# Four-layer graph network on one core: the product of negative mean and inverse root moves from VectorE to GpSimd

## The reference

```
h = max(layernorm(x), 0); x = x + L0(h, adj)   # normed = layernorm(h)*g1+be1; 8-head masked softmax(n n^T) n;
                                               # then x' = h + that; y = layernorm(x')*g2+be2; x' + gelu(y W1 + b1) W2 + b2
h = max(layernorm(x), 0); x = x + L1(h, adj)   # graph attention, 4 heads, leaky relu, masked softmax
h = max(layernorm(x), 0); x = x + L2(h, adj)   # the same form with other weights
h = max(layernorm(x), 0); x = x + L3(h, adj)   # q, k, v attention, 4 heads, Wo, relu
```

## Time and profile before

| | |
|---|---|
| time, median of 3 runs | 4204.97 us (4204.6 to 4206.16) |
| the profiled execution: time, span | 4209.86 us, 4208.1 us |
| busy: PE, DVE, ACT, POOL | 3984.2, 3210.8, 2121.9, 408.2 us (95%, 76%, 50%, 10%) |
| TensorE's granted clock over the span | 0.99 |
| one period, 2106.88 to 2233.52 us | 126.64 us, of which PE busy 123.19, DVE 99.68, ACT 66.26, POOL 12.79 |
| groups on GpSimd: `ve`, `rs`, `amx` | 192 x 514 ns, 192 x 1460 ns, 64 x 401 ns |
| VectorE's `nb` | 192 x 143 ns |

### The profile page before, as it was taken

How to read it: one execution, slowest core, us unless ns; L and a number is a source line. 1 busy time by engine, 2 the same in 40 slices (tenths; PEclk the granted TensorE clock), 3 DMA queues, 4 the chain that set the end, 5 groups by cost and what they waited for, 6 DMA issues and landing times.

```text
span 4208.1 us, 78701 instructions
## 1 busy us (share of the span) xinstructions
PE 3984.2 (95%) x32868; PEld 2119.6 (50%) x32868; DVE 3210.8 (76%) x6281; ACT 2121.9 (50%) x3297; POOL 408.2 (10%) x465
## 2 busy tenths in 40 slices
PE   5799999999999999999999999999999999999997
PEld 2455555455555455554555554555554555554553
DVE  5677778877777877777877777877778877788854
ACT  3444555544555544555544555544555544555532
POOL 0001111101111101110100110100110100110100
PEclk9899999999999999999999999999999999999998
DMA  3011111111111111111111111112111111111000
GB/s 105 24 44 51 56 36 51 34 53 52 56 36 51 31 54 54 56 36 51 31 52 56 56 36 51 31 51 56 56 31 56 31 51 56 56 31 46 21 31 31
DMA packets 212386, 195.15 MB, mean 46 GB/s; under 512 B 144448, under 2 KB 179008, under 8 KB 203584
## 3 DMA queue, kind: packets, MB, share of 16 engines
q1 hardware_dynamic: 212032, 190.12, 15.1%
HBM read 138.95 MB, written 17.56 MB: 37 GB/s over the span
## 4 chain that ended last, share of the span: by engine, by line
PE 76%; DVE 17%; ACT 4%; issue 2%; DMA 1%; SPq 0%; POOL 0%; POOLq 0%; ACTq 0%; DVEq 0%
PE M L438 11%; PE M L451 11%; DVE PG L1035 7%; PE S L539 6%; PE M L506 6%; PE O L490 6%; PE M L462 6%; PE O L555 6%; PE O L385 5%; PE S L372 4%; PE M L517 3%; PE O L495 3%; DVE PP L917 3%; PE M L596 3%; PE O L397 2%; PE M L428 2%
## 5 line engine op out<-in xcount | busy, mean ns | idle before, releaser
L639 ACT ACTIVATE PP<-S,reach 128x1024 f32<-128x1024 f32 x512 | 542.8, 1111 | 321.6 <-PE S L372 182.9
L1035 DVE SCALAR_TENSOR_TENSOR PG<-g,tcg,mT 128x512 f32<-128x512 f32 x1024 | 691.1, 742 | 12.8 <-DMA g<-t_rows 11.5
L917 DVE TENSOR_TENSOR PP<-PP,mT 128x1024 f32<-128x1024 f32 x512 | 599.6, 1218 | 22.1 <-ACT PP L639 22.1
L490 PE MATMUL O<-PG,V 128*32 128x512 f32 x4096 | 550.8, 601 | 13.8 <-DVE PG L1035 11.9
L438 PE MATMUL M<-hT,W 128*128 128x512 f32 x1024 | 461.0, 604 | 3.1 <-ACT hT L674 2.8
L451 PE MATMUL M<-W,H 128*128 128x256 f32 x2048 | 459.7, 378 | 0.0
L451 PEld LDWEIGHTS M<-W,H 128*128 128x128 f32 x2048 | 377.2, 189 | 71.7 <-issue 10.6
L1146 POOL TENSOR_SCALAR ve<-mv 128x4 f32<-128x4 f32 x192 | 98.7, 514 | 3186.1 <-DVE mv L875 3186.1
L372 PE MATMUL S<-hT 32*128 32x512 f32 x2048 | 296.6, 649 | 45.7 <-ACT PP L639 37.7
L495 PEld LDWEIGHTS O<-PG,Gp 128*32 128x32 f32 x8192 | 257.4, 110 | 140.2 <-issue 135.0
L438 PEld LDWEIGHTS M<-hT,W 128*128 128x128 f32 x1024 | 191.0, 191 | 252.4 <-issue 223.7
(11 more groups left out here) (134 smaller groups left out, 5594.7 us busy)
## 6 DMA issues: line engine op xcount, KB each, us to landing
g<-t_rows SPq DMA_DIRECT2D x64, 1024.0 KB, 4.6
adj<-adj_in SPq DMA_DIRECT2D x32, 1024.0 KB, 5.7
x<-x_in SPq DMA_DIRECT2D x32, 512.0 KB, 3.8
z<-t_rows SPq DMA_DIRECT2D x64, 256.0 KB, 3.9
out<-x SPq DMA_DIRECT2D x32, 512.0 KB, 2.9
W<-w_in SPq DMA_DIRECT2D x1, 3072.0 KB, 12.5
mT<-z SPq DMA_TRANSPOSE x128, 2.5
m<-V SPq DMA_TRANSPOSE x128, 2.5
```

Source lines behind the costliest of these rows:

```text
L490: e.matmul(k.O[0][r:r + 32, :], s.V[:, jt, 64 * hh + 32 * v:64 * hh + 32 * v + 32], p[:, u, :], start=(jt == 0), stop=(jt == NT - 1))
L639: e.activation(p[:, 2 * pair:2 * pair + 2, :], k.S[:, 2 * pair:2 * pair + 2, :], ACT.Exp, bias=k.reach[:, 7:8], scale=SC0).then_inc(k.e0.s ...
L917: e.tensor_tensor(p[:, 2 * pair:2 * pair + 2, :], p[:, 2 * pair:2 * pair + 2, :], s.mT[:, jt:jt + 1, :].to_broadcast([128, 2, N]), ALU.mul ...
L1035: e.scalar_tensor_tensor(out=p[:, u, :], in0=s.T[hh], scalar=s.tcg[:, 1, hh, jt:jt + 1], in1=s.mT[:, jt, :], op0=ALU.max, op1=ALU.mult).th ...
```

## The change

The step `nb` of VectorE is gone, with its six calls in an iteration. Its product is computed by GpSimd in the step `rs`, in two new instructions: `mn = -mean`, directly after `ve` and with no wait, and `nb = mn * rs`, after a wait for `rs`. The semaphore `rs[i]` is gone; `nb[i]` is now raised by GpSimd, and ScalarE waits for that. The wait of norm 1 for `z0` and a tile `mn` of 128 x 4 numbers are added. No other step, and no other order, is touched. The line numbers in what follows are those of the kernel before.

```diff
@@ class Dve
-    @step
-    def nb(self, b, i):
-        e, k, s = self.e, self.k, self.k.of(b)
-        if i == 0 and b >= NS:
-            self.wait_ge(*k.zr[3].at(b - NS, 3))
-        if i == 1:
-            self.wait_ge(*k.z0.at(b, 3))
-        self.wait_ge(*k.rs[i].at(b, 0))
-        e.scalar_tensor_tensor(out=s.nb[:, :], in0=s.mv[:, :, 0], scalar=-1.0, in1=s.rs[:, :], op0=ALU.mult,
-                               op1=ALU.mult).then_inc(k.nb[i].sem, 1)
@@ class Pool, def rs(self, b, i)
         self.wait_ge(*k.stat[i].at(b, 0))
         if i == 0 and b >= NS:
             self.wait_ge(*k.zr[3].at(b - NS, 3))
+        if i == 1:
+            self.wait_ge(*k.z0.at(b, 3))
         c = self.chained(e.tensor_scalar(s.ve[:, :], s.mv[:, :, 1], EPS, None, ALU.add))
+        e.tensor_scalar(s.mn[:, :], s.mv[:, :, 0], -1.0, None, ALU.mult)
         self.wait_ge(*c)
-        e.tensor_tensor(s.rs[:, :], s.ve[:, :], k.nhalf[:, :], ALU.pow).then_inc(k.rs[i].sem, 1)
+        c = self.chained(e.tensor_tensor(s.rs[:, :], s.ve[:, :], k.nhalf[:, :], ALU.pow))
+        self.wait_ge(*c)
+        e.tensor_tensor(s.nb[:, :], s.mn[:, :], s.rs[:, :], ALU.mult).then_inc(k.nb[i].sem, 1)
@@ def vector_program(do)
-        do.nb(b2, 2)
...
-        do.nb(b1, 1)
-        do.nb(b2, 3)
...
-        do.nb(b3, 5)
...
-        do.nb(b2, 4)
...
-        do.nb(b0, 0)
```

More of the change, by code:

```diff
@@ L85, in __init__ @@
         self.mT, self.m3, self.hT, self.V, self.g = rest.mT, rest.m3, rest.hT, rest.V, rest.g
-        self.st, self.mv, self.ve, self.rs, self.nb = rest.st, rest.mv, rest.ve, rest.rs, rest.nb
+        self.st, self.mv, self.ve, self.rs, self.nb, self.mn = rest.st, rest.mv, rest.ve, rest.rs, rest.nb, rest.mn
         self.stt, self.mx, self.amx, self.sh, self.tu = rest.stt, rest.mx, rest.amx, rest.sh, rest.tu
@@ L94 @@
 SIGNALS = dict(
-    mk=2, nb=(1, 0, 6), m0=16, qa=8, qa3=4, add=(4, 0, 3), nrm=(4, 0, 3), w2a=4, xx=1,
+    mk=2, m0=16, qa=8, qa3=4, add=(4, 0, 3), nrm=(4, 0, 3), w2a=4, xx=1,
     pjs=(4, 1, 3), gmx=(1, 1, 3), gex=(1, 1, 3), gv=(1, 1, 3), gm=(16, 1, 3), mx3=4, sh3=1,
@@ L104 @@
     vp=2, sqm=4, sc3=8, pv3=4, dn3=2, den3=1, rd3=1, wo=2,
-    rs=(1, 0, 6), parg=(1, 1, 3),
+    nb=(1, 0, 6), parg=(1, 1, 3),
 )
@@ L174, in __init__ @@
             s.nb = sb(f"nb{k}", [128, NT])
+            s.mn = sb(f"mn{k}", [128, NT])
             s.stt = sb(f"stt{k}", [128, NT, 8])
@@ L212, in signal @@
             return {i: Signal(sem(f"s_{name}_{i}"), per[0]) for i in range(per[1], per[2])}
-        (self.mk, self.nb, self.m0, self.qa, self.qa3, self.add, self.nrm, self.w2a, self.xx, self.pjs, self.gmx,
+        (self.mk, self.m0, self.qa, self.qa3, self.add, self.nrm, self.w2a, self.xx, self.pjs, self.gmx,
          self.gex, self.gv, self.gm, self.mx3, self.sh3, self.m3, self.ds3, self.r3, self.o3, self.woa, self.stat, self.z0,
@@ L218, in __init__ @@
          self.qt, self.sc0, self.pv0, self.dn0, self.b2r, self.tt, self.w1, self.w2, self.pj, self.srt, self.gpv,
-         self.qk, self.vp, self.sqm, self.sc3, self.pv3, self.dn3, self.den3, self.rd3, self.wo, self.rs,
+         self.qk, self.vp, self.sqm, self.sc3, self.pv3, self.dn3, self.den3, self.rd3, self.wo, self.nb,
          self.parg) = [signal(name) for name in SIGNALS]
@@ L287, in rs @@
     def rs(self, b, i): pass
-    def nb(self, b, i): pass
     def ln0(self, b, t): pass
```

## The result

| | before | after |
|---|---|---|
| time, median | 4205.05 us (4204.6 to 4206.16, 4 runs) | 4480.16 us (4477.94 to 4486.12, 4 runs) |
| ratio of the two, 95% interval | | 1.0656, 1.0638 to 1.0675 |
| profiled execution: time, span | 4209.86, 4208.1 us | 4477.94, 4476.1 us |
| TensorE's granted clock over the span | 0.99 | 0.962 |
| GpSimd busy | 408.2 us | 801.1 us |

The kernel became slower by 275 us. The forecast was slower by 41, at most 79. So the sign was right, and the size wrong by a factor of nearly 7.

The account below looks back on a forecast made before the run. TensorE was taken to bound the kernel, with 76% of the chain. Norms 3, 5 and 2 add 0.20 + 0.14 + 1.0 = 1.34 us a period, 41 us over about 31 periods, giving 4246 us, range 4206 to 4284.

Parts of the forecast that it names:

- The step that failed: Norm 5: ScalarE starts 1.14 us later, TensorE's waiting covers all but 0.14 us; +0.14 us a period.
- The rule "ends a fixed time after a start": GpSimd waits out VectorE's running two-SBUF-operand instruction; `rs` ends 0.98 us, `ve` 0.16 us after the next one starts.
- The rival "the product misses one more": Norm 2's product misses another VectorE instruction: 1.13 us more, 2.47 a period in all, 4282 us; chance 0.24.
- norm 3's product: Norm 3: ScalarE starts 0.63 us later, 0.42 us of the delay is covered; +0.20 us a period.
- Norm 2: Norm 2: GpSimd's last ordinary operation ends 1.43 us later, delaying the all-reduce and first Gelu; +1.0 us a period.
- The new wait at L472: Sign to look for: TensorE waits at L472 for ScalarE, about 1 us a period.
- The wait at L428 for `z`: Sign to look for: a new TensorE wait near L428 of 0.2 us a period.
- Cover for norms 0, 1 and 4: Norms 0, 1 and 4: ScalarE comes late enough, or waits for a DMA anyway, so delays there cost nothing.
- VectorE's slots worth nothing: Against the rival that three freed 0.15 us slots count: 0.45 a period faster, 14 us, 4191; chance 0.06.
- GpSimd doesn't slow VectorE: VectorE loses no time to GpSimd's operations: eight L1035 take 5.36 us with an `rs` among them, 5.38 without.
- its rival: GpSimd blocks VectorE 0.16 us per added operation; 0.32 a period at norm 5, 10 us on top, 4256; chance 0.04.
- The rule weighed in the prediction: Skill's rule: first issuer keeps the SBUF ports for its whole instruction; the prediction saw the trace disagree on VectorE losing time.

Follow-up runs that it names:

- the memset's trial of 0.95 us: Program that only copies x to the output: four scalar_tensor_tensor, a memset, five tensor_tensor on VectorE; GpSimd's product, issued behind the step, took 0.95 us.

## Why the prediction was right and wrong

**The step that failed** is the one on norm 5: "the product waits for the end of the first L917 (2169.15 + 1.13 = 2170.28) and ends at 2170.44". It presumed that a waiting operation of GpSimd is let in at every VectorE boundary. Up to there the chain of that norm was right: `ve`, `mn` (0.58 us; "near 0.6") and `rs` come one boundary apart. The product then comes just behind the step from the `scalar_tensor_tensor` L1035 to the `tensor_tensor` L917 and stays out through four L917 and two L927. It was given 0.14 us a period; it costs 223 to 236 us in all, over 31 periods 7.2 to 7.6 us each.

**Why the profile before didn't show it.** In the earlier trace rows every stretched operation lies inside a row of one kind: `rs` of norm 5 ends at 2168.83, before that step, and nothing of GpSimd was pending there or behind it. The change put a third dependent operation behind two others, and so moved GpSimd's last step across the boundary. The rule "ends a fixed time after a start" was read from steps C to C and A to A, and used for a step C to A. The prediction gave the product's own length bounds of "zero and the 1.04 us of `rs`", plus one VectorE instruction. Where no row shows the case, the bound is the length of the whole run behind the step: four L917 and two L927, 6.90 us (2167.59 to 2174.49 after). That alone would not have reached the time: the product would end 6.96 us behind the start of the first of them in place of 1.29, 5.67 us later, over 31 periods 176 us, which takes 4246 to 4422 and the range's upper end, 4284, to 4460. What is left of the miss, 58 us, is of the size of what TensorE's clock costs (next paragraph: 7.91 - 5.42 = 2.5 us in each of 30 periods, 75 us). The rival "the product misses one more" had the right mechanism by name, but for norm 2 and by one boundary.

**A part that was not in the sum:** 5.42 us of waiting became 8.49 in the stretch shown and 7.91 in the mean. The clock is granted at 1.2 GHz from 2173 to 2182; in the stretch shown L372 takes 0.95 us more, L385 0.74 more, and L428 1.71 more (of which ScalarE's pace, four `z` in 2.07 us, has a part).

**The size of norm 5's term.** Even with the boundary rule in force the 0.14 us was not there: with the memset ahead of the first L906 the stretch takes 7.09 us, as before. The prediction counted the idle 0.15 us ahead of L397 as all that TensorE can give there, but L397 starts 2.08 us after L385 before (2174.10 to 2176.18) and 1.74 after it with the memset (2322.90 to 2324.64), so 0.34 could be given.

**What held.**
- The boundary rule for single operations: norm 3's product ends at 2133.66, 0.15 us after the start of an L1024 at 2132.85 + 0.66. Its cost: +0.20 us a period was forecast (6 us in all), 6.6 us were measured.
- Norm 2: +1.0 us a period (31 us) against 30 measured. `mn` near 1.1 us is 1.19, the product 0.22; the all-reduce still starts some 6 us after the last ordinary operation.
- The new wait at L472 for ScalarE's Gelu exists, but is half as long as forecast: 13.8 us in 30 times with norm 5 on VectorE. The other half is spread: 9.6 us in 33 times at L428 for norm 2's ScalarE step (3.3 in two before), and the weight loads; these two make 0.65 us a period and not the whole 1.0; the rest was not followed up. The wait at L428 for `z` was to be 0.2 us a period and is 21.5 us in 66 times with the memset ahead of the first L906, against 10.8 in 4 before, 0.35 a period.
- Cover for norms 0, 1 and 4, and VectorE's slots worth nothing: 1.0003 with those three on GpSimd.
- GpSimd doesn't slow VectorE: eight L1024 take 5.39 us with a product among them, against 5.36 and 5.38. That is 0.01 over the limit that the prediction set for this, and far from the 0.16 of its rival.
- With norm 5's product let in by a memset, 36.5 us over before against the forecast of 41 (4245.35 and 4246 lie closer by luck: before was 4208.87 in these runs and 4204.97 in the prediction), and a mean period of 127.86 us against 127.9 to 128.0.

**The rule weighed in the prediction.** By the Trainium skill's rule (SBUF — State Buffer, sections Who interferes with whom and Summary: rules for kernel authors) the one that issues first keeps the ports for the whole instruction, and the other fully blocks until it finishes. VectorE isn't held by GpSimd's operations in any row read here, as the prediction said; but GpSimd is held for longer than the one instruction of the rule, up to 8.88 us over eight of them.

## What to carry to other kernels

Before a small operation is moved to GpSimd, look at what VectorE runs at the moment when the operation will be pending, kind by kind; where a row of `scalar_tensor_tensor` passes directly into `tensor_tensor`s on SBUF, take the whole remaining run as its upper bound, not one instruction, and add what TensorE's clock costs after the wait (2.5 us on 5.42 here, in the mean). An instruction of 0.15 us in VectorE's own stream is cheap; given to GpSimd, each operation of the chain can wait out a boundary of its own even without a shut-out (`mn` takes 0.23 us alone, 0.58 in norm 5 and 1.19 in norm 2). A cost rule read from a trace holds for the pairs of instructions between which it was read, and the place where a change takes it outside them belongs in the range.

## What the runs showed of the hardware

- Three or more `scalar_tensor_tensor` with two SBUF inputs, followed directly by `tensor_tensor`s on SBUF, keep a GpSimd operation that reads SBUF, and that comes in the last instruction ahead of the step or the first behind it, out until VectorE's run ends or something else comes in between: 6.54 us in the kernel, 0.93, 2.07, 3.20 and 8.88 us for 1, 2, 3 and 8 instructions. With two C it happened where semaphores were raised between them (behind two A as well) and not without; with two E, and with one C, it did not. The reverse step, from `tensor_tensor` to `scalar_tensor_tensor`, does nothing of the kind.
- A memset of 128x8 (0.07 us) at the step prevents it, and a memset, a 128x4 copy or any `scalar_tensor_tensor` later in the run ends it (2.00 to 2.08 us). A 128x4 copy or `scalar_tensor_tensor` at the step did not prevent it; in those trials the operation came after it had gone by, as it also did in the memset's trial of 0.95 us, so a memset differs from a copy there. Why is open, as is why the kind of the instructions counts at all: the runs show the conditions and not the arbiter.
- TensorE's clock: in the period shown TensorE waits from 2169.82 to 2175.24; the granted clock is 1.00 up to 2172, 0.50 (1.2 GHz) from 2173 to 2182 and 1.00 (2.4 GHz) from 2183. The stretch grew by 3.1 us more than the wait there, and by 2.5 in the mean of 29 periods.
- Between GpSimd's last ordinary operation and a partition all-reduce lie about 6 us in every kernel here (5.7 to 6.3 us of waiting that nothing in the profile names, 31 times in each).
